# Moving fp32 tanh copies and the stage sums of an RK4 recurrence from SBUF and GpSimd to PSUM and VectorE, with expert products dealt to other slots

## The reference, cut to what matters

```python
h = jnp.tanh(y @ W1.T + b1)
h = jnp.tanh(h @ W2.T + b2)
return h @ W3.T + b3          # the network f
k1 = f(y); k2 = f(y + dt / 2 * k1); k3 = f(y + dt / 2 * k2); k4 = f(y + dt * k3)
y = y + dt * (k1 + 2 * k2 + 2 * k3 + k4) / 6     # 255 times, each from the last
```

## Time and profile before

| | |
|---|---|
| three runs | 3202.09, 3207.02, 3205.28 us (median 3205.28) |
| the profiled execution: its own time | 3205.26 us |
| its span, first to last instruction | 3203.4 us |
| busy: TensorE, VectorE, ScalarE, GpSimd | 2914.3, 2374.5, 1425.9, 976.9 us |
| TensorE's clock granted, mean of the span | 0.795 of full |

### The profile page before, as it was taken

The page is one execution under the profiler, slowest core; times in us unless marked ns, Lnnn a source line. Parts: engine busy times, 40 slices in busy tenths (PEclk is TensorE's granted clock), DMA queues, the critical chain, the costliest instruction groups (busy, mean ns, idle before and its releaser), DMA issues.

```text
span 3203.4 us, 198247 instructions
## 1 busy us (share of the span) xinstructions
PE 2914.3 (91%) x77206; PEld 2405.9 (75%) x77206; DVE 2374.5 (74%) x11624; ACT 1425.9 (45%) x8958; POOL 976.9 (30%) x2171
## 2 busy tenths in 40 slices
...
PEclk8689999999999999999999666888855555555555
...
DMA packets 21976, 28.14 MB, mean 9 GB/s; under 512 B 4384, under 2 KB 12896, under 8 KB 21544
## 3 DMA queue, kind: packets, MB, share of 16 engines
...
...
## 4 chain that ended last, share of the span: by engine, by line
PE 66%; DVE 20%; ACT 8%; issue 5%; POOL 0%; DMA 0%; SPq 0%; POOLq 0%; DVEq 0%; ACTq 0%
PE PSUM L624 24%; PE PSUM L618 23%; DVE PSUM L1195 8%; PE PSUM L668 7%; PE PSUM L609 5%; DVE HA L1204 3%; DVE HB L1204 3%; ACT HA L920 2%; ACT HB L920 2%; ACT FA L921 2%; PE PSUM L698 2%; PE PSUM L642 1%; DVE AI L1200 1%; DVE UI L1207 1%; ACT FB L921 1%
## 5 line engine op out<-in xcount | busy, mean ns | idle before, releaser
L1195 DVE TENSOR_REDUCE PSUM<-PSUM 128x32 f32<-128x64 f32 x4080 | 889.9, 233 | 429.5 <-PE PSUM L624 384.6
L618 PEld LDWEIGHTS PSUM<-HA,RL 128*128 128x128 f16 x16320 | 581.5, 100 | 321.5 <-ACT HA L920 300.3
L618 PE MATMUL PSUM<-HA,RL 128*128 128x16 f16 x16320 | 734.1, 172 | 83.7 <-ACT HA L920 68.7
L920 ACT ACTIVATE HA<-PSUM 128x32 f16<-128x32 f32 x2040 | 404.2, 198 | 843.2 <-DVE PSUM L1195 843.2
L618 PE MATMUL PSUM<-HB,RLU 128*128 128x16 f16 x16320 | 732.7, 172 | 46.5 <-ACT HB L920 26.7
L920 ACT ACTIVATE HB<-PSUM 128x32 f16<-128x32 f32 x2040 | 402.6, 198 | 823.9 <-DVE PSUM L1195 823.8
L624 PE MATMUL PSUM<-HB,RHU 128*128 128x32 f16 x16320 | 694.3, 181 | 39.3 <-DVE HB L1204 38.8
L624 PE MATMUL PSUM<-HA,RH 128*128 128x32 f16 x16320 | 702.7, 182 | 28.4 <-DVE HA L1204 28.4
L618 PEld LDWEIGHTS PSUM<-HB,RLU 128*128 128x128 f16 x16320 | 571.4, 100 | 131.2 <-ACT HB L920 116.1
L624 PEld LDWEIGHTS PSUM<-HB,RHU 128*128 128x128 f16 x16320 | 574.9, 99 | 55.9 <-DVE HB L1204 50.9
L624 PEld LDWEIGHTS PSUM<-HA,RH 128*128 128x128 f16 x16320 | 575.5, 99 | 38.5 <-DVE HA L1204 34.3
...
## 6 DMA issues: line engine op xcount, KB each, us to landing
...
```

Source lines behind the costliest of these rows:

```text
L618: mm(out[m // 2][:, 2 * B * (m % 2):2 * B * (m % 2) + B], lo[:, k, m], src[:, k, 0], start=False, stop=False)
L920: A(hi[:, 2 * h:2 * h + 2, 0], src, ACT.Tanh, scale=1.0 / scale).then_inc(rk_hi, 1)
L1195: v.tensor_reduce(bank[:, SUM:SUM + 2 * B].rearrange("p (m b) -> p m b", m=2), bank[:, 0:4 * B].rearrange("p (m c b) -> p m b c", m=2, c=2 ...
```

## The change

The fp32 tanhs of both layers no longer go to SBUF tiles but into PSUM, in the same bank as their inputs (columns from `FULL`), so the low halves are formed from one PSUM and one SBUF operand. The sum over the four stages is kept by VectorE in `FS`, one instruction after each second-layer slot (a copy, two multiply-adds, and for the last stage two adds that give the high half `HSS` and the fp32 sum `SF` in PSUM); its low half is formed in slot 0 of the next step. GpSimd's `stage_sum` is gone. TensorE now waits for `rk_s` (VectorE's step of the sum) before it injects into the second layer's banks. The state is kept times 2^18 (`YB`), so that one multiply-add updates it, and GpSimd multiplies it back when it stores. The running combinations of layer 1 are rearranged so that one instruction falls away. `PER_SLOT` deals the expert products otherwise in the first step of a round: before 2, 2, 2, 1, 1, 1, 2, 1, now 0, 2, 2, 2, 1, 2, 2, 1; the second step is as before.

```diff
+FULL = 6 * B
+SCALE_Y = 2.0 ** 18
-PER_SLOT = (2, 2, 2, 1, 1, 1, 2, 1) * 2
+PER_SLOT = (0, 2, 2, 2, 1, 2, 2, 1, 2, 2, 2, 1, 1, 1, 2, 1)
...
+        AF, SF = PS[4][:, MC * B:2 * MC * B], PS[4][:, 2 * MC * B:3 * MC * B]
...
-            def stage_sum(s):
-                gp.wait_ge(rk_f, count(s, 3, 1, 1))
-                g.tensor_tensor(HS[:, :, :], FB[:, 0], FB[:, 3], ALU.add).then_inc(rk_hr, 1)
...
             def store(s):
                 gp.wait_ge(rk_y, s + 1)
-                g.tensor_copy(YS[:, :, bass.ds(s, 1)], Y[:, :].unsqueeze(2)).then_inc(rk_ys, 1)
+                g.tensor_tensor(YS[:, :, bass.ds(s, 1)], YB[:, :].unsqueeze(2), UNSCALE[:, :].unsqueeze(2), ALU.mult).then_inc(rk_ys, 1)
...
                 for j in range(4):
+                    if j or not first:
+                        pe.wait_ge(rk_s, 4 * s + j)
                     inject(1, IDV, CI[:, 3], True)
...
-                            src = PSUM[:, 2 * lay + h, SUM:SUM + 2 * B].rearrange("p (m b) -> p m b", m=2)
+                            src, full = (PSUM[:, 2 * lay + h, c:c + 2 * B].rearrange("p (m b) -> p m b", m=2) for c in (SUM, FULL))
                             A(hi[:, 2 * h:2 * h + 2, 0], src, ACT.Tanh, scale=1.0 / scale).then_inc(rk_hi, 1)
-                            A(f[:, 2 * h:2 * h + 2], src, ACT.Tanh, scale=1.0 / scale).then_inc(rk_f, 1)
+                            A(full, src, ACT.Tanh, scale=1.0 / scale).then_inc(rk_f, 1)
...
+            def summed_low():
+                TT(quad(HSS[:, :, 1]), quad(SF), quad(HSS[:, :, 0]), ALU.subtract).then_inc(rk_hs, 1)
+
+            def state(s):
+                dve.wait_ge(rk_k, s)
+                dve.wait_ge(rk_ys, s)
+                STT(YB[:, :], PS[4][:, 0:B], RB3D[:, :], YB[:, :], ALU.add, ALU.add).then_inc(rk_y, 1)
...
-                            TT(hi[:, sl, 1], f[:, sl], hi[:, sl, 0], ALU.subtract).then_inc(rk_lo, 1)
+                            TT(hi[:, sl, 1], full, hi[:, sl, 0], ALU.subtract).then_inc(rk_lo, 1)
...
-                        if lay == 1 and j == 2:
-                            if not first:
-                                state_increment(s)
-                            STT(E[:, :], DA[:, :], 1.0 / 3.0 / SCALE_U, US[:, :], ALU.mult, ALU.add).then_inc(rk_e, 1)
-                            if not first:
+                        else:
+                            if j == 0:
+                                v.tensor_copy(two(FS), FULLB).then_inc(rk_s, 1)
+                            elif j < 3:
+                                dve.wait_ge(rk_s, 4 * s + j)
+                                STT(two(FS), FULLB, 2.0, two(FS), ALU.mult, ALU.add).then_inc(rk_s, 1)
+                            else:
+                                dve.wait_ge(rk_s, 4 * s + 3)
+                                TT(quad(HSS[:, :, 0]), quad(FULLB), quad(FS[:, :]), ALU.add)
+                                TT(two(SF), FULLB, two(FS), ALU.add).then_inc(rk_s, 1)
+                            if j == 2 and not first:
                                 state(s)
```

More of the change, by code:

```diff
@@ L181, in build @@
         US = sb("US", [128, MC * B])
[L182 to L184 removed]
+        VS = sb("VS", [128, MC * B])
+        FS = sb("FS", [128, MC * B])
         Y = sb("Y", [128, B])
[L186 removed]
+        YB = sb("YB", [128, B])
+        UNSCALE = sb("UNSCALE", [128, B])
         HA, HB = sb("HA", [128, MC, 2, B], F16), sb("HB", [128, MC, 2, B], F16)
[L188 to L190 removed]
         HSS = sb("HSS", [128, MC, 2, B], F16)
@@ L237, in build @@
         rk_p, rk_r, rk_hi, rk_f, rk_lo = (sem("rk_" + k) for k in ("p", "r", "hi", "f", "lo"))
-        rk_u0, rk_ai, rk_uh, rk_u, rk_e = (sem("rk_" + k) for k in ("u0", "ai", "uh", "u", "e"))
-        rk_hr, rk_hq, rk_hs, rk_k, rk_yd, rk_y, rk_ys = (sem("rk_" + k) for k in ("hr", "hq", "hs", "k", "yd", "y", "ys"))
+        rk_u0, rk_ai, rk_uh, rk_u = (sem("rk_" + k) for k in ("u0", "ai", "uh", "u"))
+        rk_s, rk_hs, rk_k, rk_y, rk_ys = (sem("rk_" + k) for k in ("s", "hs", "k", "y", "ys"))
         o_s, o_tr, o_c, o_out = (sem("o_" + k) for k in ("s", "tr", "c", "out"))
@@ L418, in _ @@
                 store(s)
-                stage_sum(s)
             with gp.Fori(0, B) as t:
@@ L913, in step @@
                 for j in range(4):
-                    for lay, hi, f, scale in ((0, HA, FA, SCALE_U), (1, HB, FB[:, j], SCALE_V)):
-                        if j == 0 and lay == 1 and not first:
-                            act.wait_ge(rk_hr, 2 * s)
+                    for lay, hi, scale in ((0, HA, SCALE_U), (1, HB, SCALE_V)):
                         for h in range(2):
                             act.wait_ge(rk_r, count(s, j, lay, h))
-                            src = PSUM[:, 2 * lay + h, SUM:SUM + 2 * B].rearrange("p (m b) -> p m b", m=2)
+                            src, full = (PSUM[:, 2 * lay + h, c:c + 2 * B].rearrange("p (m b) -> p m b", m=2) for c in (SUM, FULL))
                             A(hi[:, 2 * h:2 * h + 2, 0], src, ACT.Tanh, scale=1.0 / scale).then_inc(rk_hi, 1)
-                            A(f[:, 2 * h:2 * h + 2], src, ACT.Tanh, scale=1.0 / scale).then_inc(rk_f, 1)
+                            A(full, src, ACT.Tanh, scale=1.0 / scale).then_inc(rk_f, 1)
                         beside(8 * r + 2 * j + lay)
@@ L1137, in _ @@
             BOTH = PSUM[:, 0:2, SUM:SUM + 2 * B]
+            FULLB = PSUM[:, 2:4, FULL:FULL + 2 * B]
             def quad(a):
@@ L1199, in step @@
                             dve.wait_ge(rk_u, 4 * s + 4)
-                            TT(AI[:, :, 1], AF[:, :, :], AI[:, :, 0], ALU.subtract).then_inc(rk_ai, 1)
+                            TT(quad(AI[:, :, 1]), quad(AF), quad(AI[:, :, 0]), ALU.subtract).then_inc(rk_ai, 1)
+                        if lay == 0 and j == 0 and not first:
+                            dve.wait_ge(rk_s, 4 * s)
+                            summed_low()
                         for h in range(2):
                             dve.wait_ge(rk_f, count(s, j, lay, h))
+                            full = PSUM[:, 2 * lay + h, FULL:FULL + 2 * B].rearrange("p (m b) -> p m b", m=2)
                             sl = slice(2 * h, 2 * h + 2)
-                            TT(hi[:, sl, 1], f[:, sl], hi[:, sl, 0], ALU.subtract).then_inc(rk_lo, 1)
+                            TT(hi[:, sl, 1], full, hi[:, sl, 0], ALU.subtract).then_inc(rk_lo, 1)
                         if lay == 0:
```

60 lines of the change are left out of this document (15 added, 45 removed).

## The result

The changed kernel takes 3100.91 us (median of four runs, 3098.56 to 3103.61) against 3205.84 for the kernel before on the same chip: a ratio of 0.9675 (95% interval 0.9658 to 0.9692), 105 us less. The forecast was 3125, so its direction and its main mechanism held, and 24 us of gain were missed. The profiled execution took 3102.6 us, its span 3100.8.

What follows compares the result with a forecast made beforehand. The prediction took the recurrence's 2040 slots, one after another through TensorE, VectorE and ScalarE, as the bound. 3205 less 64 (1.0 a round) less 15 (GpSimd's sum gone) gave 3126, rounded to 3125 us; range 3070 to 3180.

Steps and rivals of the forecast that it cites:

- Low halves from PSUM: Slots 3, 4, 7 and 9 of a round lose their stalls beside GpSimd's adds; the low half's path changes by 0.
- A: Rival: the path through PSUM is longer, delaying the low half in every slot; at 65 ns more, 3256 us; chance 0.08.
- B: Rival: GpSimd still blocks the low halves, so the stalls stay, 2.1 us a round; 3260 us; chance 0.04.
- Slot 2: In a round, a gelu waiting for the expert's third product holds the tanhs: 1.34 becomes 2.21 us, bounds 0.7 and 1.0 more.
- Slots 3 and 5: In a round, each gets a second expert product on TensorE and becomes 1.34 + 0.17 = 1.51 us.
- Slot 0: In a round, VectorE's piece sets the length: next reduce at 1.64 to 1.66 us instead of 1.77.
- Slot 7's length: In a round, two more VectorE instructions ahead of the bias copy: 1.53 us, between 1.38 (no stall) and 1.65.
- The clock: TensorE's half-rate stretches falling on slots 2 to 4 make two products a slot dearer: 0.15 us added a round.
- Rival D: More half-rate stretches of TensorE's clock follow its idle time in slots 2 and 0: 0.5 a round, 3158 us; chance 0.13.
- slots 8 to 15: Second half of a round: slots 8 and 9 take 2.69 instead of 3.17 us, the rest as before; 10.81 in all.
- GpSimd without the sum: Without GpSimd's stage sum: plain steps' slot 0 gains 6.6 us, 56 steps before the output 7, the end 1.5; together 15.

Runs made afterwards that it cites:

- the old deal's run: The changed kernel with the expert products dealt as before (2, 2, 2, 1, 1, 1, 2, 1 in both steps of a round): 3040.33 us, ratio 0.9486.

## Why the prediction was right, and where its sum was off

*Low halves from PSUM: right, and the larger part.* The pair takes 0.39 beside an add, an undisturbed slot stays 1.34 and 1.38, the low half starts 0.585 after the reduce as before. The value taken, 0, was right: 191 ns against 193 for a low half that nothing stretched. The Trainium skill's "VectorE: DVE Perf Modes" (errata section), by which the sum had been 130 us higher, does not agree with the trace, nor does "ScalarE: Activation LUTs" (Step-by-step) on a faster write to PSUM (195 after 193 ns). So rivals A and B fall. By the old deal's run this edit with the stage sum's is worth 165 us.

One part of the reading was incomplete. I put slot 7's stall down to the tanhs' low halves. On the trace before, most of it was line 1200 ahead of them, and it went because `AF` moved too, which the prediction does not mention. That slot 7 lost its stall as forecast is in part luck.

*Slot 2: the step right, its size 0.07 low.* 2.21 was forecast, 2.28 came. The third product is done at +0.44 (891.04 to 891.41 by itself), as I had it (+0.46), but the gelu starts 0.17 behind it and not 0.07: at +0.62 and not at +0.53. The next tanh comes 0.58 behind the gelu's start: +1.20 and not +1.14. In 62 rounds that is 4 us.

*Slots 3 and 5: 1.51 forecast, 1.46 and 1.45 measured.* A second product costs 0.11 there and not 0.17. *Slot 0: 1.65 forecast, 1.61 measured*, with the piece as cause.

*Slot 7's length: a mis-sized term.* I took 1.53 between 1.38 and 1.65; it is 1.38. VectorE's timeline after:

```profile
899.70 0.21 DVE L1222 TENSOR_TENSOR HSS<-PSUM,FS 128x64 f16<-128x64 f32 x1
899.83 0.22 DVE L1223 TENSOR_TENSOR PSUM<-PSUM,FS 128x64 f32<-128x64 f32 x1
899.96 0.15 DVE L1148 COPY B2E<-B 128x1 f32 x1
900.18 0.43 DVE L1186 TENSOR_REDUCE PSUM<-PSUM 128x32 f32<-128x64 f32 x2
```

The two adds of the sum and the bias copy start 0.13 apart, although each is recorded as 0.15 to 0.22 long, so three of them take 0.41 (899.70 to 900.11) and not 0.58, and the reduce waits for none of them. I had added durations where starts should be counted: 0.15 a round, 9 us in all.

*The clock: the term three times too large, its count the wrong way.* I added 0.15 a round for more stretches at the lower level. There were fewer, 5 instead of 30, with a mean granted clock of 0.99 instead of 0.97, and those five cost 0.05 a round. I counted the idle time of TensorE that the change adds in slots 0 and 2, and not that which it takes away with the stalls of slots 3 and 4. The round that I worked from had no such stretch in it (slots 5 and 6 at 1.34, slot 7 at 2.19), so the slots came out nearly as I had summed them before the addition. Rival D hardly showed in the changed kernel; in the kernel before, the new deal did cost by it (21 us).

The gap in a round, 1.40 measured against 1.0 forecast: the clock's term 0.15 (what the five stretches cost is in the slots), slot 7 0.15, slots 0, 3 and 5 0.04, 0.05 and 0.06, slot 2 -0.07, slots 8 to 15 0.05 (slot 12 had been slow as well), and -0.02 for the round of 24.38 against the mean of 24.36. The sum is 0.41. All 64 rounds gave 89.8 us (87.1 in the 62, 1.5 and 1.3 in the first and last) where 64 were forecast: 26 too little.

*GpSimd without the sum: 15 forecast, 12.8 measured for all that lies outside the 64 rounds*, 2 too much. From step 182 to the end came 7.8, where 6.6 + 1.5 were forecast, and the plain slot 0 went from 1.467 to 1.380 as forecast; 0.8 came before the first round. In the steps between (53, not 56) less came than the 7 us: the step before the statistics gave 0.6, the statistics 0.4, the convolution nothing, the output's four steps 3.0. In the convolution's rounds slots 0 and 8 did lose their stall (1.470 and 1.434 to 1.337 both), and slots 6 and 7 took it back, at a lower granted clock. The windows of the convolution's stage, before and after:

```profile
1991.80:2324.50 332.70, 319.20 (x9173) 278.08 (x9169) 249.71 (x1320) 132.00 (x1005) 83.14 (x241) 0.89 0.00 0
```
```profile
1899.80:2232.80 333.00, 321.58 (x9171) 280.62 (x9167) 260.76 (x1440) 132.15 (x1005) 27.86 (x61) 0.84 0.00 0
```
